# The new x of the first graph layer, made beside the layer's last rounds

## What is computed

```python
h = relu(layernorm(x))
x = x + attention(h, src, dst)      # layer 0: 4 heads of 32, softmax over the edges of a receiver
h = relu(layernorm(x))
x = x + message(h, src, dst, edge_attr_64, edge_weight)
# attention: t = h @ W + b;  logit = leaky_relu(<[t[src], t[dst]], alpha>)
#            out[n] = sum over edges into n of softmax(logit) * t[src] + bias
# message:   ef = (relu(ea @ We1 + be1) @ We2 + be2) * sigmoid(w @ Wt + bt)
#            out[n] = sum of relu([h[src], ef] @ Wn1 + bn1) @ Wn2 + bn2
```

## Time and profile before

| | us |
|---|---|
| median of 3 runs (2120.61 to 2124.43) | 2122.53 |
| the profiled execution | 2122.82 |
| its span, from first to last instruction | 2121.0 |
| granted TensorE clock, mean share of full speed | 0.797 |
| GpSimd busy | 1563.2 |
| TensorE / VectorE / ScalarE busy | 1524.8 / 1461.3 / 929.9 |

### The profile page before, as it was taken

The page is one execution under the profiler, slowest core; times in us unless marked ns, Lnnn a source line. Parts: engine busy times, 40 slices in busy tenths (PEclk is TensorE's granted clock), DMA queues, the critical chain, the costliest instruction groups (busy, mean ns, idle before and its releaser), DMA issues.

```text
span 2121.0 us, 47035 instructions
## 1 busy us (share of the span) xinstructions
PE 1524.8 (72%) x8785; PEld 1051.5 (50%) x8785; DVE 1461.3 (69%) x5237; ACT 929.9 (44%) x2818; POOL 1563.2 (74%) x1660
## 2 busy tenths in 40 slices
PE   6556555555555454454658998989989898898888
PEld 5434444444444343343545665656555555555556
DVE  8676767676766566565786886777767676666667
ACT  8535253535353342442466444444434443444343
POOL 7777777777777777777277777777777777777775
PEclk9766666666666666566679999999989999999999
DMA  7222222222222222222063544545544444454453
GB/s 203 54 57 57 57 57 57 58 57 57 57 58 57 56 58 57 57 56 54 22 184 107 144 144 144 145 123 146 150 128 144 144 145 144 119 146 138 133 151 105
DMA packets 111001, 213.56 MB, mean 101 GB/s; under 512 B 35214, under 2 KB 74350, under 8 KB 100723
## 3 DMA queue, kind: packets, MB, share of 16 engines
q0 software_dynamic: 51968, 107.32, 19.1%
q1 hardware_dynamic: 53031, 101.47, 16.2%
q10 hardware_dynamic: 5708, 1.77, 0.4%
HBM read 197.54 MB, written 12.88 MB: 99 GB/s over the span
## 4 chain that ended last, share of the span: by engine, by line
POOL 26%; issue 11%; PE 6%; DVE 5%; DMA 2%; ACT 1%; DVEq 1%; ACTq 0%; POOLq 0%; SPq 0%
POOL acc L1044 26%; DMA acc<-table,index 2%; PE pair L1122 1%; DVE acc L1392 1%; PE bank L1131 1%; PE pair L1116 1%; PE bank L1142 1%; DVE onehot L1350 1%; DVE pre L1374 1%; DVE ef L1357 1%; DVE x_rows L1288 0%; ACTq L1239 0%; PE bank L1073 0%; ACT msg L1223 0%; ACT hidden L1210 0%
## 5 line engine op out<-in xcount | busy, mean ns | idle before, releaser
L1044 POOL DMA_INDIRECT acc<-table,index x812 | 770.2, 949 | 252.5 <-issue 242.3
L356 POOL DMA_INDIRECT rows<-table,index x764 | 726.5, 951 | 233.0 <-issue 228.4
L812 ACT ACTIVATE rows<-rows,edge_w 128x32 f32<-128x32 f32 x1626 | 351.9, 313 | 1.1 <-issue 0.4
L504 DVE TENSOR_TENSOR acc<-acc,pair 128x256 f32 x832 | 349.2, 420 | 3.9 <-issue 2.5
L499 DVE TENSOR_SCALAR onehot<-iota_row,dst_rel 128x128 f32<-128x128 f32 x832 | 252.0, 304 | 135.2 <-PE pair L675 103.8
L1392 DVE TENSOR_TENSOR acc<-acc,bank 128x128 f32 x832 | 239.0, 287 | 143.5 <-issue 35.7
L675 PE MATMUL pair<-onehot,rows 128*128 128x128 f32 x1626 | 334.2, 367 | 0.5 <-ACT rows L812 0.5
L675 PEld LDWEIGHTS pair<-onehot,rows 128*128 128x128 f32 x1626 | 285.7, 264 | 58.9 <-issue 30.3
L1210 ACT ACTIVATE hidden<-pair,be 128x512 f32<-128x512 f32 x208 | 142.9, 687 | 380.0 <-PE pair L1122 172.4
L1131 PEld LDWEIGHTS bank<-wn1b,ef 128*128 128x128 f32 x1664 | 232.1, 202 | 109.7 <-issue 104.0
L1116 PE MATMUL pair<-ea,we 64*128 64x512 f32 x416 | 243.9, 668 | 42.4 <-DMA ea<-in_ea_t 42.4
(11 more groups left out here) (168 smaller groups left out, 1207.9 us busy)
## 6 DMA issues: line engine op xcount, KB each, us to landing
ts<-in_ts SPq DMA_DIRECT2D x52, 1024.0 KB
rows_x<-table SPq DMA_DIRECT2D x1664, 0.5 KB
ea<-in_ea_t SPq DMA_DIRECT2D x52, 512.0 KB, 5.0
rows_y<-table SPq DMA_DIRECT2D x1664, 0.5 KB
acc<-table,index POOLq DMA_INDIRECT x812
moments<-table ACTq DMA_DIRECT2D x768, 0.5 KB
rows_z<-table ACTq DMA_DIRECT2D x768, 0.5 KB
rows<-table,index POOLq DMA_INDIRECT x764
```

The lines of the kernel that those rows point to most:

```text
L356: gp.indirect_dma_start(rows0[:, n % (RING * TG), :], None, table1, bass.IndirectOffsetOnAxis(index[:, n:n + 1], 0)).then_inc(half_in[g % ...
L504: dve.tensor_tensor(acc2[:, :, ds(v, P)], acc2[:, :, ds(v, P)], both_sums[n // TG % 2][:, :, n % TG * P:(n % TG + 1) * P], ALU.add).then_i ...
L812: act.activation(row, row, ACT.Copy, scale=edge_w[:, r % 2, (g - SPANS[r][0]) * TG + t, h:h + 1]).then_inc(scaled0, 1)
L1044: gp.indirect_dma_start(rows[:, g % RG1, t, :], None, table, bass.IndirectOffsetOnAxis(index[:, n:n + 1], 0)).then_inc(gathered[g % RG1], 16)
```

## The change

In words:

- The rounds are now 4, then 24 times 8, then three of 4 groups (196 to 199, 200 to 203, 204 to 207). The maxima of round 196 are put behind groups 191 to 194; those of round 200 behind groups 197 to 199; those of round 204 stand after group 203.
- The new x is made in 13 units cut where the accumulator is closed after each of the groups 195 to 207: 2 blocks, then 4 each, then 3. The units come in three stages: 0 to 4 (ready after group 199), 5 to 8 (after 203), 9 to 12 (after 207). The steps of a stage stand between the groups of the round after it; the last stage stands behind group 207. The transposes share banks 6 and 7 in one order, each waiting for the reader of the one two before it. Everything that used banks 6 and 7 in a round moves to bank 5.
- GpSimd's own term is now added after `mix` and not before, and SyncE writes `table3` behind it, all in the first block of programs.
- ScalarE's `clear` of the accumulator stays in the second block, no longer behind the transposes, and so stands whole ahead of the first `root`.
- Tile 830 holds ten edges. GpSimd doesn't fetch it any more; SyncE fetches ten rows, in both layers. Tile 817, which ScalarE fetched in layer 0, is now fetched by GpSimd.

```diff
-SPAN_SIZES = [HALF] + [RG] * (ROUNDS - 1) + [HALF]
+SPAN_SIZES = [HALF] + [RG] * (ROUNDS - 2) + [HALF] * 3
-ACT_TILES0 = [SPANS[r][0] * TG + 1 for r in range(ACT_TURNS + 2, TURNS, ACT_TURNS)]
-EMPTY = range(-(-E // P), TILES)
+ACT_TILES0 = [SPANS[r][0] * TG + 1 for r in range(ACT_TURNS + 2, TURNS - 3, ACT_TURNS)]
+SHORT = E // P
+EMPTY = range(SHORT, TILES)
+LAST, CLOSE = TURNS - 1, TURNS - 2
+STAGES = [0, SPANS[CLOSE][0] - FIRST_END, SPANS[LAST][0] - FIRST_END, PARTS]   # 0, 5, 9, 13
+PART_SLOTS = 4
-                return (4, 5, 6, 7) if r == TURNS - 1 else ()
+                return {CLOSE - 1: (3, 4, 5, 6), CLOSE: (1, 2, 3, 3)}.get(r, ())
 SyncE, first block
+                    sp.wait_ge(agg0, SHORT // TG - RING + 1)
+                    ... ten one-row DMAs into rows0 ...
+                    for u in range(PARTS):
+                        sp.wait_ge(own, u + 1)
+                        sp.dma_start(table3[...], x_rows[:, blocks_of(u), :]).then_inc(x1_out, 16)
 GpSimd, first block
+                        gp.wait_ge(cb_ready, stage_of(u) + 1)
+                        gp.tensor_tensor(heads(mine), heads(mine), per_head(own_scale, u, SH), ALU.mult).then_inc(owned, 1)
+                        gp.wait_ge(owned, u + 1)
+                        gp.wait_ge(mixed, u + 1)
+                        gp.tensor_tensor(x_rows[...], x_rows[...], mine, ALU.add).then_inc(own, 1)
 VectorE, behind the first of the three short rounds
+                            link(dve.tensor_copy(sums_t[:, :, LCOL:], logit[:, :, SH:]))
+                            for u in range(5):
+                                gather_stats(u)
+                            maxima_of(0)
 VectorE, from group 200 on
+                    shares(0)
+                    sum_group(g0, at[0:TG]);          penalties(LAST);          scaled_sums(0)
+                    sum_group(g0 + 1, at[TG:2 * TG]); keep_row_penalties(LAST); scaled_sums(1); mix(0)
+                    sum_group(g0 + 2, ...);           scaled_sums(2);           mix(1)
+                    sum_group(g0 + 3, ...);           mix(2); scaled_sums(3)
+                    scan_rows(LAST); mix(3); scaled_sums(4); scan_row_ends(LAST); mix(4); full_maxima(LAST)
+                    for u in range(5, 9): gather_stats(u)
+                    maxima_of(1); at = first_of(g1); rescale(LAST, at); shares(1)
+                    sum_group(g1, ...);     scaled_sums(5)
+                    sum_group(g1 + 1, ...); scaled_sums(6); mix(5)
+                    sum_group(g1 + 2, ...); scaled_sums(7); mix(6)
+                    sum_group(g1 + 3, ...); gather_stats(9); scaled_sums(8)
+                    for u in range(10, 13): gather_stats(u)
+                    maxima_of(2); mix(7); mix(8); shares(2)
+                    scaled_sums(9); scaled_sums(10); mix(9); scaled_sums(11); mix(10); scaled_sums(12); mix(11); mix(12)
 TensorE, from group 200 on
+                    sum_group(CLOSE, g0);     turn_penalties(LAST); turn_sums(0); turn_sums(1)
+                    sum_group(CLOSE, g0 + 1); turn_sums(2)
+                    sum_group(CLOSE, g0 + 2); turn_sums(3)
+                    sum_group(CLOSE, g0 + 3); turn_logits(LAST); turn_sums(4); turn_row_ends(LAST); turn_carries(LAST)
+                    turn_stats(5); turn_stats(6); turn_weights(LAST); turn_stats(7); turn_stats(8)
+                    sum_group(LAST, g1);      turn_sums(5)
+                    sum_group(LAST, g1 + 1);  turn_sums(6)
+                    sum_group(LAST, g1 + 2);  turn_sums(7); turn_stats(9)
+                    sum_group(LAST, g1 + 3);  turn_sums(8)
+                    ... turn_stats(10 to 12), turn_sums(9 to 12) ...
 ScalarE, second block
                     def clear(u):
-                        act.wait_ge(s_t, u + 1)
 SyncE, second block
+                        sp.wait_ge(radd, SHORT // TG - RG1 + 1)
+                        ... ten one-row DMAs into rows, ahead of the last load of ea and ts ...
```

More of the change, by code:

```diff
@@ L22 @@
 UNITS = -(-NB // UB)
-EARLY = 3
 TG = 4
@@ L540, in _ @@
+                    for r in range(1, LAST):
                         span = groups(r - 1)
@@ L560, in _ @@
                                     full_maxima(r)
[L561 to L566, removed]
+                        at = first_of(groups(r)[0])
+                        if not parts_after(r):
+                            scan_rows(r)
+                            scan_row_ends(r)
+                            full_maxima(r)
@@ L570, in _ @@
                     dve.wait_ge(biased, NB)
+                    shares(0)
+                    g0 = SPANS[CLOSE][0]
+                    sum_group(g0, at[0:TG])
+                    penalties(LAST)
+                    scaled_sums(0)
+                    sum_group(g0 + 1, at[TG:2 * TG])
+                    keep_row_penalties(LAST)
+                    scaled_sums(1)
+                    mix(0)
+                    sum_group(g0 + 2, at[2 * TG:3 * TG])
+                    scaled_sums(2)
+                    mix(1)
@@ new lines, in _ @@
+                    sum_group(g0 + 3, at[3 * TG:4 * TG])
+                    mix(2)
+                    scaled_sums(3)
+                    scan_rows(LAST)
+                    mix(3)
+                    scaled_sums(4)
+                    scan_row_ends(LAST)
+                    mix(4)
+                    full_maxima(LAST)
+                    for u in range(5, 9):
+                        gather_stats(u)
+                    maxima_of(1)
+                    g1 = SPANS[LAST][0]
+                    at = first_of(g1)
@@ new lines, in _ @@
+                    dve.wait_ge(acc0, g1 * TG)
+                    rescale(LAST, at)
+                    shares(1)
+                    sum_group(g1, at[0:TG])
+                    scaled_sums(5)
+                    sum_group(g1 + 1, at[TG:2 * TG])
+                    scaled_sums(6)
+                    mix(5)
+                    sum_group(g1 + 2, at[2 * TG:3 * TG])
+                    scaled_sums(7)
+                    mix(6)
+                    sum_group(g1 + 3, at[3 * TG:4 * TG])
+                    gather_stats(9)
@@ new lines, in _ @@
+                    scaled_sums(8)
+                    for u in range(10, 13):
+                        gather_stats(u)
+                    maxima_of(2)
+                    mix(7)
+                    mix(8)
+                    shares(2)
+                    scaled_sums(9)
+                    scaled_sums(10)
+                    mix(9)
+                    scaled_sums(11)
+                    mix(10)
+                    scaled_sums(12)
+                    mix(11)
+                    mix(12)
@@ L641, in turn_carries @@
                         for way in range(2):
-                            last = pe.matmul(bank[7][0:n, way:way + 1], runs[SPANS[r][1]][:, way, 2 * way:2 * way + n], ident[0:1, 0:1], start=True, stop=True)
+                            last = pe.matmul(bank[5][0:n, CARRY + way:CARRY + way + 1], runs[SPANS[r][1]][:, way, 2 * way:2 * way + n], ident[0:1, 0:1], start=True, stop=True)
                         last.then_inc(carry_turned, 1)
@@ L682, in _ @@
                     turn_weights(0)
[L683 to L685 removed]
+                    for r in range(1, LAST):
+                        for k, g in enumerate(groups(r - 1)):
                             sum_group(r - 1, g)
[L687 to L688 removed]
                             if k == 0:
@@ L995, in line, with tail @@
                             sp.dma_start(rows_y[o + q:o + q + 1, j % LINE_SLOTS, :], table2[ds(row, 1), :]).then_inc(line1_in[j % LINE_SLOTS], 16)
+                    def tail():
+                        sp.wait_ge(radd, SHORT // TG - RG1 + 1)
+                        for o in range(0, E % P, BATCH):
+                            fill = min(BATCH, E % P - o)
+                            sp.load(regs[0:fill], line_index1[0:1, len(LINE_TILES1) * P + o:len(LINE_TILES1) * P + o + fill])
+                            for q, v in enumerate(regs[0:fill]):
+                                row = sp.snap(v, min_val=0, max_val=N - 1)
+                                sp.dma_start(rows[o + q:o + q + 1, SHORT // TG % RG1, SHORT % TG, :], table2[ds(row, 1), :]).then_inc(tail1_in, 16)
                     def rows_of(table, u):
@@ L1001, in _ @@
                     load(1)
-                    for u in range(UNITS):
-                        sp.wait_ge(mixed, u + 1)
-                        sp.dma_start(rows_of(table3, u), x_rows[:, blocks(u), :]).then_inc(x1_out, 16)
                     for u in range(UNITS):
```

309 lines of the change are left out of this document (177 added, 132 removed).

## The result

The changed kernel takes 2133.82 us (median of 4, 2132.20 to 2135.07) against 2121.96 (median of 4, 2120.61 to 2124.43) for the kernel before: a ratio of 1.0057, interval 1.0045 to 1.0069. It is slower by 11.9 us. Forecast were 2124.5 and a range up to 2132.0; the time lies above both.

What follows compares the result with a forecast made beforehand. GpSimd's fetches were taken to bound each layer. Layer 1's start hardly moves (1089.1 against 1089.48), later waits leave GpSimd 2.6 us later, one fetch less gives back 0.6: 2.0 later, 2124.5, range 2115.5 to 2132.

Steps and rivals of the forecast that it cites:

- The step that failed: End of the first block: last write issued at 1086.5, engines met after 0.55 + 0.55, next block begins at 1087.6.
- Steps 1 to 7: VectorE from groups 188 to 195 through the short rounds and tail: last `mix` at 1085.0 against 1086.86 before.
- the cancellation behind it: End of layer 0: the 14.8 us of waiting won are mostly paid back by two more round boundaries.
- The first `root`: ScalarE in layer 1: table load, one root and 13 clears come first, so it starts at 1095.8, 7.8 later.
- The stop: Layer 1 before group 8: GpSimd has its 32 fetches issued at 1129.1 and waits 1.4 us for `table2`.
- The second stop: Layer 1 before group 12: GpSimd waits 1.4 us more, for the ring's first sender add at 1152.1.
- The tile less: Tile 830, one GpSimd fetch less in layer 1: worth between 0 and 1.25 us, taken as 0.6.
- Slow TensorE: Rival: TensorE stays slow, VectorE waits at every group from 200; last `mix` at 1092, total 2131; chance 0.17.
- Fast TensorE: Rival: TensorE runs fast and waits between groups go; last `mix` at 1079, total 2118.5, taken together 2117; chance 0.20.
- Masks blocked by GpSimd: Rival: GpSimd's 13 products each hold up a VectorE mask, 8 us in all; total 2129; chance 0.08.
- step 5: Boundary before group 204: exposed maxima of the last round with `mix`, `scaled_sums`, reductions and shares; 12.4 us, to 1060.1.
- Clears hidden: Rival: `table2` and the first add come in time, the 2.6 us shrink to -0.4, total 2121.5; chance 0.08.

Runs made afterwards that it cites:

- experiment 1: Changed kernel with the first block closed without GpSimd's drain; ratio 1.0011 to the kernel before, +2.3 us.
- experiment 4: Changed kernel with an extra GpSimd drain right behind the last fetch of layer 0; ratio 1.0015 to the kernel before, +3.2 us.
- experiment 3: Kernel before with one tiny GpSimd clear of four columns behind the last add of layer 0; ratio 1.0041, +8.7 us.
- experiment 8: Kernel before with the three short rounds alone, x still made in the second block; ratio 1.0030, +6.4 us.
- experiment 5: Changed kernel without GpSimd's first-block drain, ScalarE's 13 clears moved into the first block; ratio 1.0010 to the kernel before.
- experiment 9: Changed kernel without GpSimd's first-block drain, tile 830 of layer 1 fetched by GpSimd again; ratio 1.0016 to the kernel before.
- experiment 2: Kernel before with the first block closed without GpSimd's drain; ratio 1.0002.

## Why the prediction was wrong, step by step

**The step that failed** is "The block begins when the last write is issued and the engines have met: 1086.5 + 0.55 + 0.55 = 1087.6." The meeting was priced as two small moments. It has one member that needs 9 us, GpSimd. The forecast's own sign of being wrong, a first fetch after 1094, came. Counting the steps of the start of layer 1, forecast 1089.1 and measured 1099.05: the last `mix` 1.8 later than forecast, GpSimd's lag behind it 2.4 and not 1.5 (+0.9), the write and its landing 2.3 and not 2.6 (-0.3, with the 2.33 of experiments 1 and 4), the drain 7.5 that the sum didn't have. The 7.5 are what the drain adds beyond the landing of the last write: 1099.05 against 1089.24 + 2.33. Experiments 1, 3 and 4 show it three ways, by taking it out, by exposing it alone, and by moving it.

The row could have been read before: L287 holds a drain of 23.9 us on GpSimd, and the earlier trace rows show GpSimd idle from 1022.3 to 1060.1 around it. The prediction put the own term where GpSimd had nothing to fetch. There was room for it; what had no more room was the drain that the idle time covered.

**Steps 1 to 7** held, one by one. Ends forecast and measured: group 195 at 1004.4 and 1005.0; round 196 with its maxima 1022.0 and 1023.0; the boundary before group 200 1030.6 and 1032.3; group 203 1047.7 and 1049.1; the boundary before 204 1060.1 and 1063.3; group 207 1072.8 and 1075.2; the last `mix` 1085.0 and 1086.8. The errors never pass 3.2 us, and the last two legs gained 1.4 back. Experiment 8 bears out the cancellation behind it.

**The first `root`** came 7.8 us behind the block's start (1098.4 to 1106.2), forecast 8.2 (1087.6 to 1095.8), with the clears in one piece of 6.5 (forecast 6.7). From the first fetch to the landing of `table2` it is 41.7 us, forecast 41.4. That the clears cause the stop before group 8 fell with experiment 5: without them `table2` lands as late, behind the 3 MB. **The stop** was forecast at 1.4 and is 2.24 less the usual 0.30 of issue, 1.9. **The second stop**, at the ring, was forecast at 1.4 and did not come: group 12's gap is 0.32, though its release is VectorE's add and no longer the issue. Fetches and add arrive together. (Two of the working's figures here are 0.1 to 0.2 off: 1129.1 + 1.4 is 1130.5 and not 1130.7, and 1152.1 is 2.5 behind 1149.57 and not 2.6. Nothing hangs on it.)

**The tile less** was put at 0.6 us won. In the profiled executions the last fetch is 10.0 us later than before, and the span is 12.3 longer; the end is 17.1 behind the last fetch for 14.8. That is +2.3, of which a fetch less would explain 1.25. But the same distance is 16.6 and 16.3 in experiments 2 and 3, which have the fetches of the kernel before, so most of the 2.3 is within what executions differ by. What the tile is worth stays open (experiment 9).

Together: start +9.6, stop +1.9, one fetch -1.25, end +2.3 make 12.5, of 12.3 in the span. Without the drain the changed kernel is at +2.3 (experiment 1) or +3.2 (experiment 4), each give or take 2. That agrees with the forecast's +2.0 for all the rest, but that it is so close is partly luck: the start came later than its -0.4 even without the drain (1091.6 would be +2.1), the second stop of 1.4 did not come, and the 0.6 for the tile was never seen.

**The rivals.** *Slow TensorE* gave 2131, near the time, for a reason that isn't the one. It had the last `mix` at 1092. The windows from group 196 to the last `mix` (columns as in the earlier trace rows) show a mean granted clock, by length, of 0.66, and of 0.71 from 1031 on, over the groups 200 to 207 and the tail that its mark of 0.6 was set for:

```profile
1004.00:1023.00 19.00, 12.09 (x76) 9.22 (x76) 14.79 (x61) 5.60 (x28) 13.73 (x15) 0.59 0.25 55
1023.00:1031.00 8.00, 6.75 (x36) 5.85 (x37) 2.67 (x15) 3.42 (x18) 0.00 (x0) 0.50 0.00 2
1031.00:1047.00 16.00, 9.71 (x73) 7.06 (x72) 12.64 (x46) 4.51 (x22) 1.64 (x4) 0.73 0.03 9
1047.00:1060.00 13.00, 6.27 (x37) 4.84 (x37) 10.34 (x31) 2.42 (x11) 4.47 (x7) 0.61 0.29 83
1060.00:1072.00 12.00, 11.11 (x77) 9.00 (x77) 9.98 (x32) 5.51 (x27) 1.93 (x3) 0.71 0.01 4
1072.00:1087.00 15.00, 5.09 (x30) 3.79 (x30) 13.49 (x32) 0.30 (x1) 7.76 (x10) 0.79 0.30 85
```

*Fast TensorE* is out by the same rows: the boundary before group 200, a chain of short operations, ran at 0.50, and the last `mix` came at 1086.8 and not at its 1079.

*Masks blocked by GpSimd* was right as a mechanism and too dear. Two masks of VectorE, and the operations of GpSimd beside them:

```profile
1047.13 0.51 DVE L569 TENSOR_SCALAR onehot<-iota_row,dst_rel 128x128 f32<-128x128 f32 x1
```

```profile
1046.83 0.73 POOL L425 TENSOR_TENSOR x_rows<-x_rows,feat 128x256 f32<-128x256 f32 x1 [2.32 <-DVE x_rows L652]
...
1063.36 0.62 POOL L422 TENSOR_TENSOR feat<-feat,rows 128x256 f32<-128x256 f32 x1 [7.92 <-DVE rows L639]
```

The mask at 1047.13 ends at 1047.64, GpSimd's add at 1047.56. The mask at 1063.33 (shown above, 0.73 for the usual 0.28) ends at 1064.06, GpSimd's product at 1063.98. At 1032.28, 1044.30 and 1047.89 it is the same: each mask ends 0.08 to 0.09 us behind GpSimd's operation. The Trainium skill, "SBUF — State Buffer", section "Who interferes with whom", has it that the second to come is fully blocked. The trace after agrees for three of these five. The masks at 1032.28 and 1063.33 are recorded 0.03 us ahead of GpSimd's operation and were held all the same, and three more masks overlapped one of its operations (1043.23, 1043.76, 1046.61) and took the usual 0.27 to 0.28, the one at 1043.76 although it came second. Beyond 0.28 each the five cost 1.0 us together, where 8 had been set for all 13 products.

The masks are not all of it. Three operations of the exposed maxima of the last round also stand beside GpSimd's:

```profile
1050.66 0.77 DVE L530 TENSOR_TENSOR_SCAN seg_max<-pen_b,fore 34x128 f32<-34x128 f32 x1
...
1052.92 0.61 DVE L538 TENSOR_TENSOR_SCAN runs<-pens,edge_of 1x36 f32<-1x36 f32 x1
...
1054.87 0.71 DVE L551 SCALAR_TENSOR_TENSOR top<-tail_pen,bank,with_prev 34x128 f32<-34x128 f32 x1
```

In the round before, with no tensor operation of GpSimd near, they took 0.42, 0.20 and 0.35 us. That is 1.1 us on the path, and step 5 was 1.8 longer than forecast (14.2 for 12.4). The prediction had priced masks alone. Nor is "a mask beside fetches 0.28 or 0.29" the whole of it: of 41 masks from 800 to 845 in the trace before, with fetches running, 11 took 0.33 to 0.48.

*Clears hidden* is out: there is a stop before group 8 in every version that keeps the order of SyncE's loads.

## What to carry to other kernels

Before moving work across the end of a block, or onto an engine that was done early, look at each engine's drain at that line and at when it ran: idle time ahead of a meeting point can be hiding one. If an engine with indirect fetches must work late in a block, drain it right behind its last fetch, where it idles anyway (experiment 4). And when a stop is removed, name what arrives just behind it: here the clears, the queue of loads and the ring followed each other within some 3 us, and each repair passed the wait on.

## What the runs showed of the hardware

GpSimd's drain (812 fetches or more before it) ends 8.9 us behind the end of its last instruction, whether that was a fetch (kernel before, experiment 4), the last of 26 tensor operations (changed kernel) or a clear of 0.10 us that came 33 us after the last fetch (experiment 3). A second drain, with only tensor operations since the first, took 0.69 us and ended 0.1 us behind the last of them. The 8.9 us are the same behind 812 fetches (both blocks of the kernel before) and behind 1623 without a drain between (experiment 1); fewer weren't tried. VectorE, ScalarE and SyncE drained in 0.02 to 2.5 us at the same lines.

Short operations of VectorE took longer beside a tensor operation of GpSimd: scans 0.77 for 0.42 us and 0.61 for 0.20, a mask 0.73 for 0.28.
